# An FFN's residual updates: from two engines, one per expert step, to the vector engine alone, two per early step

## What is computed

```python
def _L0_ffn_ref(x, gate_w, expert_w):
    scores = jnp.einsum('bsh,eh->bse', x, gate_w)
    chosen = jnp.argmax(scores, axis=-1)
    onehot = jax.nn.one_hot(chosen, gate_w.shape[0], dtype=x.dtype)
    expert_out = jnp.einsum('bsh,efh->bsef', x, expert_w)
    return x + jnp.einsum('bsef,bse->bsf', expert_out, onehot)

x = L0_attn_x
x = x + 0.5 * _L0_ffn_ref(_layernorm(x, axis=-1), L0_ffn_gate_w, L0_ffn_expert_w)
x = x + _L0_attn_ref(_layernorm(x, axis=-1), L0_attn_Wqkv, L0_attn_Wout, L0_attn_bout)
x = x + 0.5 * _L0_ffn_ref(_layernorm(x, axis=-1), L0_ffn_gate_w, L0_ffn_expert_w)
```

## Time and profile before

| | us |
|---|---|
| median of 2 timed runs | 2552.34 |
| lowest and highest of them | 2536.91, 2567.76 |
| the profiled execution | 2541.11 |
| its span on the slowest core (core 1) | 2539.6 |
| spans of the 8 cores | 2522.1 to 2539.6 |
| mean granted TensorE clock of the 8 cores | 0.792 to 0.797 of full speed |

### The profile page before, as it was taken

How to read it: one execution, slowest core, us unless ns; L and a number is a source line. 1 busy time by engine, 2 the same in 40 slices (tenths; PEclk the granted TensorE clock), 3 DMA queues, 4 the chain that set the end, 5 groups by cost and what they waited for, 6 DMA issues and landing times.

```text
span 2539.6 us, 27915 instructions; the slowest of 8 cores (2522.1 to 2539.6 us)
## 1 busy us (share of the span) xinstructions
PE 2053.8 (81%) x9872; PEld 1033.5 (41%) x9872; DVE 854.0 (34%) x1704; ACT 447.3 (18%) x1059; POOL 400.4 (16%) x511
## 2 busy tenths in 40 slices
PE   3686768998987389968977996899595989898983
PEld 0672223443446143423433442434491434343462
DVE  2203113243333443345234424533303233333242
ACT  2200000000000115513740461165400000000000
POOL 0000112424335200000000000000000115151533
PEclk9557989999999595678568657956655999999996
DMA  7005996545456651012001100100002555544565
GB/s 196 1 1 124 195 206 159 170 132 150 141 139 210 139 133 40 1 39 101 1 34 67 40 1 34 67 1 16 27 1 53 150 147 155 149 150 133 158 191 207
DMA packets 78117, 257.60 MB, mean 101 GB/s; under 512 B 9232, under 2 KB 20496, under 8 KB 73888
## 3 DMA queue, kind: packets, MB, share of 16 engines
q0 software_dynamic: 57648, 203.28, 30.2%
q1 hardware_dynamic: 20336, 52.55, 6.9%
HBM read 249.27 MB, written 33.63 MB: 111 GB/s over the span
## 4 chain that ended last, share of the span: by engine, by line
PE 75%; DMA 9%; DVE 8%; issue 3%; ACT 2%; POOL 1%; SPq 0%; DVEq 0%; POOLq 0%; ACTq 0%
PE pdf L93 36%; PE pss L93 11%; PE pq L93 5%; PE pgf L93 5%; PE pspt L98 4%; PE pv L93 4%; DMA webuff<-wexpT 4%; PE pbf L93 3%; PE pso L93 2%; DMA webuff<-wexp_bf 2%; DMA x_sb<-xT 2%; PE pba L93 1%; DVE xc_at L104 1%; DMA wexp_bf<-webuff 1%; DVE qraw_at L104 1%
## 5 line engine op out<-in xcount | busy, mean ns | idle before, releaser
L93 PE MATMUL pdf<-lmbuff,webuff 128*128 128x512 bf16 (+1 forms) x5120 | 1037.1, 366 | 136.7 <-DVE lmbuff L104 78.8
L93 PEld LDWEIGHTS pdf<-lmbuff,webuff 128*128 128x128 bf16 x5120 | 508.7, 100 | 665.0 <-issue 186.1
L104 DVE TENSOR_TENSOR lmbuff<-xcf,mkbuff 128x1024 bf16<-128x1024 bf16 (+1 forms) x320 | 216.1, 685 | 664.7 <-PE pdf L93 650.5
L150 POOL DMA_DIRECT2D webuff<-wexp_bf x288 | 154.4, 537 | 969.4 <-PE pdf L93 792.5
L125 ACT CAST ev8f<-pdf 128x1024 bf16<-128x1024 f32 (+1 forms) x20 | 17.6, 930 | 1402.4 <-PE pdf L93 1402.4
L111 DVE TENSOR_SCALAR pn_bf_at<-p_at,rc_at 128x384 bf16<-128x384 f32 x256 | 95.9, 417 | 240.3 <-PE pspt L98 233.0
L141 ACT ACTIVATE p_at<-pss,negc_at 128x384 f32<-128x384 f32 x256 | 147.8, 590 | 36.0 <-PE pss L93 35.5
L93 PE MATMUL pss<-biasq_sb,idb 128*128 128x384 bf16 x256 | 128.3, 501 | 15.3 <-DVE k_sb_at L104 15.3
L93 PE MATMUL pss<-k_sb_at,q_sb_at 64*128 64x384 bf16 x256 | 127.5, 498 | 0.0
L93 PE MATMUL pgf<-gwT_sb,x_sb 128*128 128x8 f32 x576 | 123.2, 361 | 0.0
L93 PEld LDWEIGHTS pgf<-gwT_sb,x_sb 128*128 128x128 f32 x576 | 123.0, 333 | 0.0
(11 more groups left out here) (120 smaller groups left out, 1552.5 us busy)
## 6 DMA issues: line engine op xcount, KB each, us to landing
webuff<-wexp_bf POOLq DMA_DIRECT2D x288, 512.0 KB, 5.0
webuff<-wexpT POOLq DMA_DIRECT2D x32, 512.0 KB, 15.6
wexp_bf<-webuff SPq DMA_DIRECT2D x32, 512.0 KB, 10.3
wbufA_at<-wqkv_bf POOLq DMA_DIRECT2D x6, 2048.0 KB, 9.0
wbufB_at<-wqkv_bf POOLq DMA_DIRECT2D x6, 2048.0 KB, 8.3
x_sb<-xT SPq DMA_DIRECT2D x8, 1152.0 KB, 22.7
mkbuff<-onehot_sc SPq DMA_DIRECT2D x64, 128.0 KB, 5.9
outT<-x_sb SPq DMA_DIRECT2D x8, 1024.0 KB, 11.0
```

What stands on the lines that cost most here:

```text
L93: E.matmul(a, b, c, start=st, stop=sp, tile_position=tp),
L104: eng, lambda E, o=out, x=a0, y=a1, op=op: E.tensor_tensor(o, x, y, op),
L150: eng, lambda E, o=out, i=in_: E.dma_start(o, i), inc=sem, n=16)
```

## The change

Two edits. All residual units run on DVE, and the two halves of the scratch `uscr` alternate between even and odd d. In experts 0 to 3 a second pending unit is emitted right behind the first one, so the 8 units of a tile are emitted in experts 0 to 3, two at each, and none in experts 4 to 7. POOL's list keeps the weight loads and has no TENSOR_TENSOR left. After the last tile of a block all 8 units run on DVE.

```diff
             def emit_phase2_d(d, t0, w, p1cnt, p1acnt):
-                eng = "dve" if d < 4 else "pool"
-                sl_ = 0 if d < 4 else 1
+                eng = "dve"
+                sl_ = d % 2
                 us = uscr[:, sl_ * 512: sl_ * 512 + w]
                 b.wait(eng, "dve", p1cnt)
                 b.wait(eng, "act", p1acnt)
@@ -483,6 +483,9 @@
                 b.wait("pe", "pool", ph2["pool"])
                 for e in range(8):
                     if pending:
+                        cc, eng = pending.pop(0)()
+                        ph2[eng] = cc
+                    if e < 4 and pending:
                         cc, eng = pending.pop(0)()
                         ph2[eng] = cc
                     if e == 5 and ti + 1 < len(tcs):
```

## The result

| | before | changed |
|---|---|---|
| median, us | 2539.56 (12 runs) | 2556.19 (13 runs) |
| lowest and highest, us | 2533.05, 2577.93 | 2549.39, 2599.07 |
| profiled execution, us | 2541.11 | 2560.96 |

The ratio of the changed kernel to the one before is 1.0079, 95% interval 1.0051 to 1.0108: slower by 13 to 27 us, a real loss, and under 2%. The kernel before had a median of 2552.3 us over its first two runs and has 2539.6 over twelve. Ratios here use only runs with all cores undisturbed. The forecast was +15.3 us.

What follows compares the result with a forecast made beforehand. PE waits for DVE's `lmbuff` at tile boundaries and for POOL-issued weights in 256-token last tiles. Boundaries +25.5, tails +6.2, last tiles -16.4 sum to +15.3 us on 2541.1: 2556.4 us, range 2538 to 2584.

Steps and rivals of the forecast that it cites:

- Boundary: At 8 tile boundaries a second DVE unit delays the first `lmbuff` product PE waits for: 3.19 us each, +25.5 us.
- Clock after a longer idle: After each boundary, 3.2 us more PE idle adds 0 slow-clock time, at most 0.2 us (1.6 us in all).
- Experts 1 to 3: In 256-token last tiles, two DVE units make PE wait 0.4 us before experts 2 and 3: +1.6 us in all.
- Experts 4 to 7 and the last tiles: Without POOL's units ahead of weight loads, last tiles gain 10.6 and 5.8 us: -16.4 us, DVE waits included.
- The rule that the second half repeats the stops of the first: In last tiles, second-half stops were assumed equal to the first half's: 2.44 us in block 0, 0.25 in block 1.
- Tail: After each block's last matmul, 32 ops run alone on DVE, 16.9 us against 13.76: +3.1 us per block, +6.2 us.
- Sum: Whole kernel: +25.5 + 6.2 - 16.4 = +15.3 us on the profiled 2541.1 us, 0.6% slower.
- stream limit: Rival in the last tiles: weight bandwidth keeps the second-half stops, so no gain there; 2574 us, chance 0.16.
- Delay through DVE's units: Rival: DVE's residual ops delay POOL's descriptor work, so last-tile loads land late in experts 1 to 3; 2568 us, chance 0.06.
- Slow tail: Rival in the block tails: DVE ops stay at 0.76 us, +27.5 us over both blocks; 2578 us, chance 0.06.
- Free unit at the boundary: Rival: PE's restart is already held by something as late, so the second unit costs nothing; 2531 us, chance 0.04.

Runs made afterwards that it cites:

- units from expert 1 on: The changed kernel with its two units per step moved one expert later, to experts 1 to 4, none at expert 0: 2497.69 us, ratio 0.9837.
- the first edit alone: The changed kernel without the second pending unit: all residual units on DVE, one at each of experts 0 to 7; 2526.97 us, ratio 0.9951 to the kernel before.
- the run with SP's loads: The kernel before, with the weight loads of each block's last tile issued by SP instead of POOL: 2533.87 us, ratio 0.9994.

## Why the prediction was right, point by point

- *Boundary, 8 x 3.19 = +25.5.* Right: six times 9.65 - 6.46 = 3.19, one 9.38 - 6.20 = 3.18, and 2.83 in front of block 0's last tile, where the idle had been 6.55 and not 6.20. That makes +25.2 us. The run with units from expert 1 on shows it the other way round.
- *Clock after a longer idle, 0 with 0.2 as the bound.* Right: PE's time for tiles after 9.65 us of idle is 112.1 to 113.6 us (115.4 and 115.5 once each on two cores), and 112.0 to 113.4 after 6.46 us in the kernel before; without the two outliers the averages over all cores are 112.97 and 112.88 us. What was not foreseen is the other direction: after 3.21 us of idle the clock sometimes stays up.
- *Experts 1 to 3, 0.4 us twice per last tile.* 0.40 and 0.56 us. The second is longer than my 0.4: on core 1 DVE works without a gap from expert 2's first product at 2461.38 to expert 3's at 2469.09, 7.71 us, and PE needs 7.15 us for an expert. My term (1.6 us) should have been 1.9.
- *Experts 4 to 7 and the last tiles, -16.4.* On core 1 7.1 + 9.2 = 16.3 us, over the eight cores 8.0 + 6.7 = 14.7 us. That core 1's sum meets the forecast to 0.1 us is luck. Its halves were off in opposite ways: block 0 gained 7.1 where I had 5.8, block 1 9.2 where I had 10.6. The rule that the second half repeats the stops of the first is borne out no closer than that, and the cores lay further apart than these differences already before the change (67.8 to 76.3 us in block 0). The working has a slip of its own as well: the 58.9 us contain block 1's first half as it ran, stops included, so its 0.25 us are counted twice in each block, 0.5 us in all. The mechanism is shown by three runs: the stops move with POOL's units, vanish when the loads leave its queue, and stay away when the units run on POOL again at a later point, with the loads still on SP.
- *Tail, +6.2.* Measured 16.8 - 13.8 = 3.0 per block, +6.1. The 0.76 us was contention: the op takes 425 ns alone and 760 ns beside POOL at 256 tokens and, in the run with SP's loads, 0.69 and 1.57 us at 512. The rule that the Trainium skill's page "SBUF — State Buffer" gives in "Who interferes with whom", that a DVE instruction with two SBUF inputs contends with a GpSimd instruction that reads SBUF, agrees with these numbers.
- *Sum +15.3.* On core 1 the terms add to 25.2 - 16.3 + 6.1 = +15.0. The core's span grew by 8.6 us only (2539.6 to 2548.2): its first tile of block 0, which no edit touches, ended 3.8 us earlier (before the restarts at 392.62 and 392.01, less 6.46 and 9.64 us of idle), and its tiles of 512 tokens took some 3 us less in all. Other cores went the other way. Such differences between executions are as large as single terms here. Over the eight cores the terms add to 25.2 - 14.7 + 6.1 = +16.6 us, and the mean span grew by 18.2 us (2530.1 to 2548.3). The ratio over all runs, +0.5 to +1.1% or 13 to 27 us, holds the sum, with its middle at 20. That the median of the changed kernel, 2556.19 us, lies 0.2 us from the forecast of 2556.4 is luck.

The rivals: stream limit, with no gain in the last tiles, out (the run of the first edit alone). A small part of it was true and in my sum: with half the loads about 6 us more are gained. Delay through DVE's units: not seen, since loads landed in 5.2 us beside them and in 5.8 without, and block 1's last tiles show no stop for weights of 2 us. That agrees with what the Trainium skill's page "SBUF — State Buffer" infers in "Who interferes with whom", that `tensor_tensor` does not keep GpSimd from writing descriptors. A smaller delay is not ruled out: four cores stop for 0.9 to 2.1 us after expert 1 of block 0's last tile, but up to 2.0 us was lost there before the change too. Slow tail, out. Free unit at the boundary, out.

Left open: why block 0's last tile keeps more stops than block 1's on most cores, with the same loads (some 2.4 us of waits for weights against 1.0 on core 1, and 62.9 against 61.7 us of length over the eight cores). No run separated the two.

## What to carry to other kernels

Before moving work off an engine, ask in which queue position it hurts, not how busy the engine is: POOL's units cost some 15 us here because weight loads stood behind them, and a DVE unit cost 3.2 us where it stood in front of the product that restarts the matrix engine, and a pair of them at most 0.6 us elsewhere in the loop. Count each unit of work against the next instruction in its queue that someone waits for, and put it right behind that instruction; here that turned a loss of 0.8% into gains of 2.1 and 2.6% with the same operations. And when a transfer leaves a queue, look at what its waits had been holding back.

## What was not expected of the hardware

- After 3.21 us of idle PE sometimes restarts at 2.4 GHz and sometimes at 1.2: two tiles of the same execution took 110.67 and 112.35 us. After 6.46 us of idle in the kernel before, and 9.65 in the changed one, no tile took less than 112.0 us, and after 1.48 + 0.54 us 37 of 40 tiles ran in 110.82 us.
- Two engines with f32 ops of two SBUF inputs slow each other. In the run with SP's loads 128x512 goes from 0.69 to between 1.45 and 1.57 us on DVE, while POOL's goes from between 1.15 and 1.27 to between 1.42 and 1.71, and 128x256 from 0.42 to 0.76 us on DVE while POOL's takes 0.67 to 0.72. They do not simply take turns: at 512 columns a pair passes every 1.6 us, where the two ops alone add to 1.9. Splitting 32 ops of 256 columns over both took 13.8 us instead of 16.8, 18% less and not half.
